# A decoder layer in fp32 on one core: attention probabilities transposed by half rows, and three steps moved

## The reference

```python
x = x + attn(layernorm(x))            # 16 heads of 32, rotary q and k, causal softmax, @ Wo.T
x = x + xattn(layernorm(x), ctx)      # 32 heads of 16, axial rotary q and k, no mask, @ Wout + bout
x = x + ffn(layernorm(x))             # silu(gate) * up, hidden 1408, dequantised integer weights

def attn_core(q, k, v):               # per head
    scores = q @ k.T * scale          # 128 x 128
    return softmax(scores) @ v
```

## Time and profile before

| What | Value |
|---|---|
| median of 3 runs | 1757.78 us (1755.44 to 1758.74) |
| the profiled execution, its own time | 1756.11 us |
| its span from the first to the last instruction | 1754.3 us |
| PE busy | 1671.0 us (95%) |
| DVE busy | 1161.3 us (66%) |
| ACT busy | 980.4 us (56%) |
| POOL busy | 486.7 us (28%) |
| mean granted TensorE clock | 0.989 |
| matmuls L461 of prob, 1536 of them | 189.2 us busy, 277 ns mean |

### The profile page before, as it was taken

The page is one execution under the profiler, slowest core; times in us unless marked ns, Lnnn a source line. Parts: engine busy times, 40 slices in busy tenths (PEclk is TensorE's granted clock), DMA queues, the critical chain, the costliest instruction groups (busy, mean ns, idle before and its releaser), DMA issues. The chain is left out here.

```text
span 1754.3 us, 37254 instructions
## 1 busy us (share of the span) xinstructions
PE 1671.0 (95%) x13120; PEld 1357.5 (77%) x13120; DVE 1161.3 (66%) x2111; ACT 980.4 (56%) x3824; POOL 486.7 (28%) x473
## 2 busy tenths in 40 slices
PE   5999999999999999999999999997899999999997
PEld 4777787777778787787778777775688888888885
DVE  7787777877778777787777777766553444434432
ACT  5567676766767667676666767665432222222221
POOL 4233333334333343333343333331010110110011
PEclk9999999999999999999999999997999999999999
DMA  5011110111001110001110010020601120210210
GB/s 205 28 30 30 35 29 29 39 41 35 29 29 31 50 35 29 29 29 52 31 32 29 29 51 29 22 76 7 222 27 47 72 71 0 72 72 0 72 48 25
DMA packets 55095, 80.95 MB, mean 46 GB/s; under 512 B 4880, under 2 KB 25488, under 8 KB 55056
## 3 DMA queue, kind: packets, MB, share of 16 engines
q1 hardware_dynamic: 55056, 80.43, 14.2%
HBM read 63.63 MB, written 16.78 MB: 46 GB/s over the span
## 5 line engine op out<-in xcount | busy, mean ns | idle before, releaser
L700 ACT ACTIVATE prob<-bank,nmax 128x128 f32<-128x128 f32 x1536 | 538.8, 406 | 204.4 <-DVE nmax L873 204.4
L700 ACT ACTIVATION_READ_ACCUMULATOR prob<-bank,nmax 128x1 f32 x1536 | 378.3, 246 | 0.0
L873 DVE TENSOR_REDUCE nmax<-bank 128x4 f32<-128x512 f32 x384 | 240.8, 683 | 120.5 <-PE bank L500 101.5
L1199 PE MATMUL fbank<-shared,piece_hi 128*128 128x512 f32 x1152 | 280.3, 394 | 0.0
L1199 PEld LDWEIGHTS fbank<-shared,piece_hi 128*128 128x128 f32 x1152 | 215.8, 187 | 53.2
L391 POOL TENSOR_TENSOR rope_buf<-rope_buf 128x512 f32<-128x512 f32 x128 | 167.2, 1306 | 238.0 <-DVE rope_buf L830 237.8
L476 PE MATMUL bank<-shared,z1T_h 128*128 128x512 f32 x768 | 203.4, 406 | 4.5 <-ACT shared L683 2.6
L1351 DVE SCALAR_TENSOR_TENSOR h<-fbank,su_c,sil 128x512 f32<-128x512 f32 x88 | 66.0, 750 | 206.2 <-PE fbank L1199 199.0
L461 PE MATMUL bank<-ident,prob 128*128 128x128 f32 x1536 | 189.2, 277 | 5.5 <-ACT prob L700 5.5
L461 PEld LDWEIGHTS bank<-ident,prob 128*128 128x128 f32 x1536 | 174.9, 143 | 12.8 <-ACT prob L700 8.4
L476 PEld LDWEIGHTS bank<-shared,z1T_h 128*128 128x128 f32 x768 | 140.1, 189 | 47.9 <-issue 14.8
(11 more groups left out here) (157 smaller groups left out, 2921.7 us busy)
## 6 DMA issues: line engine op xcount, KB each, us to landing
xA<-in_x SPq DMA_DIRECT2D x32, 256.0 KB, 3.0
xB<-in_x SPq DMA_DIRECT2D x32, 256.0 KB, 2.9
x_scratch<-x SPq DMA_DIRECT2D x32, 256.0 KB, 2.0
shared_loaded<-x_scratch SPq DMA_DIRECT2D x8, 1024.0 KB, 7.7
xr<-x_scratch SPq DMA_DIRECT2D x8, 1024.0 KB, 5.6
out<-xr SPq DMA_DIRECT2D x8, 1024.0 KB, 4.3
cx<-in_ctx SPq DMA_DIRECT2D x32, 128.0 KB, 2.3
range_window<-in_wg SPq DMA_DIRECT2D x27, 112.0 KB, 2.0
```

Source lines behind the costliest of these rows:

```text
L700: last = nc.scalar.activation(prob[:, c, i, :], S[c][:, i * P:(i + 1) * P], ACT.Exp, bias=nmax[:, c, i:i + 1], accum_out=rs[:, h:h + 1])
L873: nc.vector.tensor_reduce(out=nmax[:, c, :], in_=S[c][:, :].rearrange("p (g k) -> p g k", g=G), op=ALU.max, axis=AX, negate=True).then_inc ...
L1199: last = nc.tensor.matmul(dst[:, :], w[:, k, cols], z[:, k, :], start=(n == 0), stop=(n == len(passes) * KT - 1))
```

## The change

A set's transposes become 32 matmuls of 64 columns where they were 16 of 128. Each 128 x 128 block is transposed as an upper and a lower half of its rows: rows 0 to 63 use the upper half of the array's rows, rows 64 to 127 the lower half (tile size 64 x 128, tile positions 0 and 64). The matmuls alternate between the halves, and the two neighbours write two different banks. For a pair of banks (0 and 1, 2 and 3) a first round does the upper half of one and the lower half of the other, a second round (`swap`) the halves that are left; it waits, by the new semaphore, for the first round of the same pair to have ended. A pair of banks is reported done as a whole, so the even copies wait for a count that is one higher.

Moved in the order: on TensorE, v2's projection goes from ahead of the transposes of q2 and set 1 to behind them, and the transpose of rbc1 from ahead of collect to behind attend1 (ScalarE follows: v2's copies go behind the odd copies of set 1, and the copy rT1 behind the first bank's exponentials of set 2a). On VectorE, the normalisation of the self attention's context goes behind all four row maxima of set 2a, the range scan from behind z2's normalisation to behind the rotary operations of q1, and the inversion of set 2's row sums behind the even copies of set 2b.

```diff
             def transpose_prob(u, q):
-                for c in range(G):
-                    pe.wait_ge(p_r[kind(u)], G * nth(u, q) + c + 1)
-                    transpose4(S[c], lambda i, c=c: prob[:, c, i, :]).then_inc(pT_d[kind(u)], 1)
+                k = kind(u)
+                for swap in range(2):
+                    for pair in range(2):
+                        if swap == 0:
+                            pe.wait_ge(p_r[k], G * nth(u, q) + 2 * pair + 2)
+                        else:
+                            pe.wait_ge(cross_d[k], 2 * nth(u, q) + pair + 1)
+                        pe.sem_inc(gate, 1)
+                        for i in range(G):
+                            for half, rows in enumerate(HALVES):
+                                c = 2 * pair + (half ^ swap)
+                                last = nc.tensor.transpose(S[c][:, i * P + rows.start:i * P + rows.stop],
+                                                           prob[rows, c, i, :], ident[rows, rows])
+                        if swap == 0:
+                            last.then_inc(cross_d[k], 1)
+                        else:
+                            last.then_inc(pT_d[k], 2)
...
                 if has_c:
+                    pe.wait_ge(rot["q2"], cq + 1)
+                    transpose4(PA, columns(RA["q2"])).then_inc(rT_d["q2"], 1)
+                if has_s:
+                    transpose_prob("1", sq)
+                if has_c:
                     if has_o:
                         pe.wait_ge(riT_r[2], oq + 1)
                     project(TC, cxT_h, cxT_l, "kv2", CKT, slice(D, 2 * D)).then_inc(pj["v2"], 1)
-                    pe.wait_ge(rot["q2"], cq + 1)
-                    transpose4(PA, columns(RA["q2"])).then_inc(rT_d["q2"], 1)
-                if has_s:
-                    transpose_prob("1", sq)
-                if has_s and has_c:
-                    pe.wait_ge(rb_r[1], sq + 1)
-                    pe.wait_ge(v2_r, cq + 1)
-                    transpose4(TC, columns(rbc1[:, :, :].rearrange("p h d -> p (h d)"))).then_inc(ri_d[1], 1)
...
                     attend1()
-                if is_first(sq):
-                    pe.wait_ge(rb_r[1], 1)
+                if has_s:
+                    pe.wait_ge(rb_r[1], sq + 1)
+                    if has_c:
+                        pe.wait_ge(v2_r, cq + 1)
                     transpose4(TC, columns(rbc1[:, :, :].rearrange("p h d -> p (h d)"))).then_inc(ri_d[1], 1)
...
             def even_copies(u, q):
                 for c in (0, 2):
-                    dve.wait_ge(pT_d[kind(u)], G * nth(u, q) + c + 1)
+                    dve.wait_ge(pT_d[kind(u)], G * nth(u, q) + c + 2)
...
                 if has_c:
-                    row_maxima("2a", cq, (0, 1))
+                    row_maxima("2a", cq, range(G))
                 if has_s:
                     dve.wait_ge(riT_r[1], sq + 1)
                     dve.wait_ge(av_d[1], sq + 1)
                     normalise_ctx(1, PC, rT1)
-                if has_c:
-                    row_maxima("2a", cq, (2, 3))
                 if has_n and has_c:
                     rope("q1", nx, PA, DK1, cos1, sin1, DK1 ** -0.5)
+                if in_loop:
+                    dve.wait_ge(rng_in, 48 * (cq - 1))
+                    nc.vector.tensor_reduce(out=rng[:, bass.ds(cq - 2, 1)], in_=window[:, :, :].rearrange("p a n -> p (a n)"),
+                                            op=ALU.max, axis=AX, apply_absolute_value=True).then_inc(rng_r, 1)
```

More of the change, by code:

```diff
@@ L242, in attention_phase @@
         pT_d = {n: sem(f"prob{n}T_done") for n in (1, 2)}
+        cross_d = {n: sem(f"prob{n}T_first_quarters_done") for n in (1, 2)}
         pTe_r = {n: sem(f"prob{n}T_even_ready") for n in (1, 2)}
@@ L290, in head @@
             return 2 * (G * j + c) + odd
+        HALVES = (slice(0, P // 2), slice(P // 2, P))
         ORDER = [w[0] for w in WSRC]
@@ L592, in turn @@
                 if has_c:
-                    if has_o:
-                        pe.wait_ge(riT_r[2], oq + 1)
-                    project(TC, cxT_h, cxT_l, "kv2", CKT, slice(D, 2 * D)).then_inc(pj["v2"], 1)
                     pe.wait_ge(rot["q2"], cq + 1)
@@ L599, in turn @@
                     transpose_prob("1", sq)
-                if has_s and has_c:
-                    pe.wait_ge(rb_r[1], sq + 1)
-                    pe.wait_ge(v2_r, cq + 1)
-                    transpose4(TC, columns(rbc1[:, :, :].rearrange("p h d -> p (h d)"))).then_inc(ri_d[1], 1)
+                if has_c:
+                    if has_o:
+                        pe.wait_ge(riT_r[2], oq + 1)
+                    project(TC, cxT_h, cxT_l, "kv2", CKT, slice(D, 2 * D)).then_inc(pj["v2"], 1)
                 if has_s:
@@ L722, in turn @@
                 if has_c:
+                    act.wait_ge(rT_d["q2"], cq + 1)
+                    nc.scalar.activation(flat(qT2), PA[:, :], ACT.Copy).then_inc(rT_r["q2"], 1)
+                if has_s:
+                    odd_copies("1", sq)
+                if has_c:
                     act.wait_ge(pj["v2"], cq + 1)
@@ L726, in turn @@
                     nc.scalar.activation(v2o[:, :, 1, :], v2p[:, :, 1, :], ACT.Copy).then_inc(v2_r, 1)
-                    act.wait_ge(rT_d["q2"], cq + 1)
-                    nc.scalar.activation(flat(qT2), PA[:, :], ACT.Copy).then_inc(rT_r["q2"], 1)
+                    exponentials("2a", cq, (0,))
                 if has_s:
-                    odd_copies("1", sq)
                     act.wait_ge(ri_d[1], sq + 1)
@@ L736, in turn @@
                 if has_c:
-                    exponentials("2a", cq)
+                    exponentials("2a", cq, (1, 2, 3))
                     odd_copies("2a", cq)
@@ L971, in turn @@
                     normalise(2, x1A, z2, sq)
[L972 to L975, removed]
                 if has_c and not has_s:
@@ L987, in turn @@
                 if has_c:
+                    even_copies("2b", cq)
+                if has_c:
                     dve.wait_ge(p_r[2], 2 * G * (cq + 1))
@@ L990, in turn @@
                     nc.vector.reciprocal(rinv2[:, :], rsum2[:, :]).then_inc(ri_r[2], 1)
-                if has_c:
-                    even_copies("2b", cq)
                 if nz is not None and has_s:
```

## The result

| | median us | runs | ratio to before, 95% interval |
|---|---|---|---|
| before | 1756.82 | 4 (1755.44 to 1758.74) | |
| the change | 1714.45 | 4 (1713.79 to 1716.51) | 0.976 (0.974 to 0.978) |

What follows compares the result with a forecast made beforehand. TensorE, 97% busy, was taken as the bound, with uncovered copies leaving gaps. Savings of 0.63 and 0.89 us make 1.52 a turn, times 31 turns 47 us; 1756.1 becomes 1709, plus 1.7 gives 1711 us, range 1694 to 1738.

Steps and rivals of the forecast that it cites:

- The turn: One turn of the loop: 35.31 us forecast against 36.83 before, a gain of 1.52 us.
- S, the set: Time of one set's transposes of prob after the change: 1.35 us (1.1 to 1.7) against 1.74.
- the stream: Inside a set: both row halves work side by side, 16 x 54 ns = 0.87 us.
- the cross wait: Inside a set: a pair's second round waits for its first, costing 0.25 us (0 to 0.4).
- The change of shape: Tile shape changes ahead of and behind a set: 0.25 us for the pair (0.2 to 0.4).
- the wait of 0.4 us ahead of scores2a: After set 1 and the value projection, PE waits some 0.4 us for VectorE's copies; scores2a start at 12.4.
- Set 2b's end: From set 2b's transposes to the next turn: 0.89 us a turn saved, scan and reciprocal gone from ahead of the copies.
- 31 turns: Whole program: 1.52 us saved in each of 31 turns with both attentions, 47 us; turns at the ends add nothing.
- a clock below 1.00: TensorE's granted clock: if sets are short and it falls below 1.00, the sum is wrong in an unpriced way.
- Rival 1: In the sets: transposes gain nothing, the moves do; a set stays about 1.74 us; 1735 us; chance 0.24 shared.
- Rival 2: Inside each set: halves do not run side by side, a set takes 2.2 us; slower, 1777 us; chance 0.12.
- Rival 3: The chain of scores, copies and exponentials binds, 0.8 us a turn given back; 1735 or 1720 us; chance 0.24 shared.

Runs made afterwards that it cites:

- e3: The changed kernel with the half transposes reordered: all upper halves of a bank pair first, then all lower, so neighbours share an array half; 1778.06 us, 1.012.
- e8: The changed kernel with both rounds of banks 0 and 1 in a row, then both of 2 and 3; 1764.46 us, 1.005.
- e10: The changed kernel with rotated q as a fifth bank in sets 1 and 2a, and VectorE's even copies of set 1 ahead of reciprocals and z1's normalisation; 1707.83 us, 0.972.
- e4: The changed kernel with the range scan back behind z2's normalisation; 1731.81 us, 0.986.
- e6: The changed kernel with the reciprocals of set 2's row sums ahead of the copies of 2b again; 1717.99 us, 0.978.
- e1: The changed kernel with whole 128-column transposes again, bank by bank, all moves kept; 1734.85 us, 0.988.
- e12: The changed kernel with VectorE's even copies of set 1 ahead of its reciprocals and z1's normalisation, no fifth bank; 1728.72 us, 0.984.
- e9: The changed kernel with the eight transposes of z1 and z2 behind set 2b's also done by half rows; 1722.66 us, 0.981.
- e13: The changed kernel with set 1's even copies first on VectorE, then z1's normalisation, then set 1's reciprocals; 1715.30 us, 0.977.

## Why the prediction was right, point by point

- **The turn.** 35.31 us were forecast, 35.25 measured; every mark in the table above lies within 0.2 us. The only late one is set 1's start, by 0.15: the step from the whole transposes of q2 to the half ones takes 0.59 (633.67 to 634.26) where 0.44 had been. The largest misses are scores2b and the transposes of 2a, 0.19 and 0.17 early, for the reason given under set 1.
- **S, the set.** 1.35 us forecast; 1.26 from its first start to the next row, and 0.15 or 0.1 ahead of it: about 1.4. The parts were off and made up for each other, so that the total came out is in part luck. The term that was too small is the stream: a pair of halves takes 62 ns and not 54, so sixteen take 1.0 us and not 0.87. The overlap was right, but 54 was half of a whole one's 109, and e3 shows that a half alone takes 62 too. The term that was too large is the cross wait, 0.1 (634.75 to 634.88, where 0.06 is the usual step) and not 0.25, since the other pair's round of 0.25 covers most of its 0.3 (e8). The change of shape costs the 0.25 that was said: 0.15 or 0.1 ahead, and some 0.1 behind, where the next row starts 0.15 us after the last half and the halves 0.03 after each other.
- **Set 1: the wait of 0.4 us ahead of scores2a did not come.** The projection ends only at about 637.0, since the set began 0.15 later than forecast and the projection's first piece takes 0.56 us instead of 0.47, and the copies at 635.84 + 1.22 = 637.06. I had said 12.0 and 12.3; it was 12.2 and 12.2. That S hardly matters in set 1 was thus wrong: there is no slack left. e10, where set 1's transposes and q2's are shorter, fits that.
- **Set 2b's end.** 0.89 us behind the transposes were forecast; 3.51 became 2.65, 0.86. e4 and e6 divide it. Over the 28 turns from the fourth mask product to the last a turn takes 35.76 us with the scan back, 35.31 with the reciprocals back and 35.23 in the change: 0.53 and 0.09. The scan (0.85) thus showed by three fifths and the reciprocals (0.34) by a quarter, where the forecast took both whole.
- **The sum over the program: the step that failed is "31 turns", with "the turns at the ends add nothing that I count".** The first masks stand at 25.97, 57.00, 93.30, 129.48 us before and at 25.98, 57.53, 94.80, 131.52 after: the first three turns got 2.0 us longer. The 28 that follow gain 44.1 (1030.41 against 986.34 to the mask of the last one), 1.57 each. And from that last mask to the end of the span it takes 596.8 us where it took 594.4. So 44.1 - 2.0 - 2.4 = 39.6 us, the difference of the spans.

  The granted clock accounts for most of the first part. The third of these turns before, in the change, and in e4, which differs from the change inside the loop alone, and so not in this turn (the clock stands ahead of the last two columns):

```profile
93.30:129.48 36.18, 35.77 (x340) 29.33 (x341) 27.77 (x52) 24.82 (x111) 13.43 (x13) 1.00 0.12 37
```

```profile
94.80:131.52 36.72, 36.43 (x389) 28.46 (x389) 27.96 (x53) 24.99 (x113) 13.46 (x13) 0.95 0.12 37
```

```profile
95.17:130.39 35.22, 34.93 (x388) 27.25 (x389) 27.95 (x53) 24.79 (x113) 13.44 (x13) 1.00 0.13 38
```

  The same work takes 35.22 us at 1.00 and 36.72 where the mean is 0.95, with a stretch in it at the lower of the two levels, 1.2 GHz. So 1.5 us were lost to the clock there. The turn ahead of it has 0.95 too (37.27 us; before, 36.30 at 1.00); what part of that is the clock's was not separated. The prediction had named a clock below 1.00 as a thing that it had not priced. Why the clock fell here and not before stays open: in the 10 us from 90 to 100, in which it fell, PE was busy for 7.99 us, and before, at 1.00, for 8.12.

  In the last turns a pair of banks waits for both banks' exponentials: in the change the last 24 matmuls of such a set start together once the last exponential is there, and the scores follow 2.50 us later (1171.11 to 1173.61), where the last four whole ones were followed by the scores after 1.90 (1212.70 to 1214.60). From scores2a to those scores it takes 10.82 us (from 1162.79) where it took 9.64 (from 1204.96).
- **Rival 1** (the transposes gain nothing) falls by e1: 20 us above the change, on the 1735 that this rival had. **Rival 2** was wrong in its premise: e3. That e3, which makes the premise true, came to 1778 where the rival had 1777 is luck: it had 0.7 us a turn, and e3's turn is 0.25 longer than before (37.08 against 36.83), so 8 us in the 28 turns; the other 12 lie in the first turns (the fourth mask at 135.36, before 129.48) and behind the last mask (600.9 us, before 594.4). **Rival 3** (the chain binds) has a grain in it: with the copies' chain level with the banks within 0.1 us and TensorE's own work done only 0.2 earlier, small shifts on VectorE (e6, e12) and at the turn's end (e9) show at once.

## What to carry to other kernels

Two savings that attack a pipeline's bound and its waits are worth more together than apart (22 and 11 us, and 42 in one): a shorter step on the busiest engine pays in full only once its waits are covered. Row tiling pays by its neighbours: alternate the halves (here into different banks; one bank was not tried), and put other work between a round and the one that must wait for it. And before small operations of VectorE are moved, look at what POOL starts at that moment.

## What the runs showed of the hardware

- Half-row transposes take 62 ns from start to start, whether one alone (e3) or two side by side in different halves (the change): the second is free. Against the 109 ns of a whole one that is a gain of 1.75 and not 2, since halving the columns does not halve the time.
- A wait of TensorE for its own matmul, with nothing between, costs 0.3 us a time (e8: six a turn, 50 us on the kernel).
- VectorE's operation on 128x1 grew from 0.16 to 0.87 us beside one of POOL's (e12), and shrank back when POOL's began later (e13). The same stood in the kernel before: its L809, 64 times, took 158 ns at least, 585 in the middle and 1041 at most; at 639.82 it took 1.03 us beside POOL's operation of 639.55 to 640.84. The change leaves it so (L827: 159, 587 and 1039 ns); at 620.28 it takes 1.03 us, ahead of kT2.
- The granted clock of the same turn was 1.00 in one kernel and 0.95 in another, and the turn 1.5 us longer with it (e4 and the change, above).
